# Cross attention heads woven into a causal attention's pairs, and PSUM values of two attentions copied by ScalarE

## What is computed

```python
x = _layernorm(x + _L0_attn_ref(x, ...))        # bucketed linear attention
x = _layernorm(x + _L0_xattn_ref(x, ctx, ...))  # two softmax attentions, 16 heads of 32, with feed-forward: "a1", "a2"
x = _layernorm(x + _L0_ffn_ref(x, ...))         # 16 experts, 4 chosen
x = _layernorm(x + _L1_attn_ref(x, ...))        # causal, 16 heads of 64: "l1"
x = _layernorm(x + _L1_xattn_ref(x, ctx, ...))  # cross attention, 16 heads of 8: "lx"
x = _layernorm(x + _L1_ffn_ref(x, ...))         # 8 experts, 2 chosen, with a capacity
```

## Time and profile before

| | us |
|---|---|
| median of 3 runs | 814.76 |
| lowest, highest | 813.08, 826.92 |
| the profiled execution | 812.73 |
| its span in the trace | 810.9 |
| TensorE's mean granted clock in it | 0.934 |

### The profile page before, as it was taken

How to read it: one execution, slowest core, us unless ns; L and a number is a source line. 1 busy time by engine, 2 the same in 40 slices (tenths; PEclk the granted TensorE clock), 3 DMA queues, 4 the chain that set the end, 5 groups by cost and what they waited for, 6 DMA issues and landing times.

```text
span 810.9 us, 16176 instructions
## 1 busy us (share of the span) xinstructions
PE 726.4 (90%) x5744; PEld 537.8 (66%) x5744; DVE 492.8 (61%) x1309; ACT 413.1 (51%) x1047; POOL 290.0 (36%) x398
## 2 busy tenths in 40 slices
PE   5559898899998999999999989989898899999986
PEld 3336476665756566699888877857576445667665
DVE  3557798877869588254543446545445658674653
ACT  2215357565665576754544448655563544454311
POOL 0013455554556467320000008333331555454300
PEclk9959799999999999899999999999999656899999
DMA  7563343624427374000000000001010520000000
GB/s 238 156 140 74 87 95 78 149 52 110 109 53 190 85 174 159 2 1 1 1 1 1 1 1 4 1 1 36 6 40 5 171 82 26 9 2 8 8 7 7
DMA packets 25174, 48.10 MB, mean 59 GB/s; under 512 B 7264, under 2 KB 14192, under 8 KB 25096
## 3 DMA queue, kind: packets, MB, share of 16 engines
q1 hardware_dynamic: 24376, 45.66, 21.9%
q10 hardware_dynamic: 720, 1.41, 0.5%
HBM read 17.49 MB, written 0.52 MB: 22 GB/s over the span
## 4 chain that ended last, share of the span: by engine, by line
PE 62%; DVE 15%; issue 10%; ACT 7%; POOL 3%; DMA 2%; SPq 1%; POOLq 0%; DVEq 0%; ACTq 0%
PE G L522 8%; PE SC L772 7%; PE SC L759 7%; PE SC L702 5%; PE G L563 4%; PE SO L745 3%; DVE shift_cols L1471 3%; PE SC L794 3%; PE G L871 3%; ACT causal_probs L1085 2%; PE SO L826 2%; PE SC L678 2%; PE G L527 2%; PE SM L719 2%; PE G L585 2%
## 5 line engine op out<-in xcount | busy, mean ns | idle before, releaser
L1100 ACT ACTIVATE exps<-SC 128x512 f32<-128x512 f32 x192 | 114.2, 596 | 112.6 <-PE SC L702 112.0
L1471 DVE TENSOR_REDUCE shift_cols<-SC 128x2 f32<-128x512 f32 x192 | 129.7, 683 | 35.5 <-PE SC L678 34.6
L1550 POOL TENSOR_TENSOR rstd<-variance,consts 128x2 f32<-128x2 f32 (+1 forms) x48 | 37.2, 775 | 286.6 <-DVE variance L1164 283.7
L1619 POOL TENSOR_TENSOR VB<-exps 128x256 f32<-128x256 f32 x128 | 95.0, 749 | 65.1 <-ACT exps L1100 64.4
L1074 ACT ACTIVATE hidden<-SC,cols 128x256 f32<-128x256 f32 x128 | 53.5, 470 | 66.3 <-PE SC L759 66.1
L1641 POOL TENSOR_TENSOR causal_probs<-causal_probs,inverse 128x256 f32<-128x256 f32 x64 | 51.6, 828 | 70.5 <-DVE inverse L1484 70.5
L1505 DVE SCALAR_TENSOR_TENSOR R<-SC,small,R 128x128 f32<-128x128 f32 x128 | 39.0, 346 | 55.6 <-PE SC L772 55.0
L1085 ACT ACTIVATE causal_probs<-SC,negmax 128x128 f32<-128x128 f32 (+1 forms) x128 | 52.2, 423 | 37.2 <-DVE negmax L1479 37.0
L702 PE MATMUL SC<-stacked_q,stacked_k 100*128 100x256 f32 x256 | 66.5, 343 | 4.5 <-DMA stacked_q<-shift_rows 3.0
L772 PEld LDWEIGHTS SC<-ffn_w,hidden 128*128 128x128 f32 x512 | 66.0, 192 | 5.3 <-issue 1.8
L678 PE MATMUL SC<-stacked_k,stacked_q 96*128 96x256 f32 x256 | 56.6, 308 | 12.7 <-DVE shift_cols L1471 7.4
(11 more groups left out here) (244 smaller groups left out, 1500.1 us busy)
## 6 DMA issues: line engine op xcount, KB each, us to landing
stacked_k<-k_hi SPq DMA_DIRECT2D x64, 128.0 KB, 2.3
stacked_q<-q_hi SPq DMA_DIRECT2D x64, 128.0 KB, 2.4
ffn_w<-in_ffn_w SPq DMA_DIRECT2D x16, 512.0 KB, 4.6
stacked_k<-k_lo SPq DMA_DIRECT2D x32, 128.0 KB, 2.4
stacked_q<-q_lo SPq DMA_DIRECT2D x32, 128.0 KB, 2.4
packed_k<-U SPq DMA_DIRECT2D x48, 32.0 KB, 1.9
packed_q<-YN SPq DMA_DIRECT2D x48, 32.0 KB, 1.9
a_weights<-in_a_li SPq DMA_DIRECT2D x3, 256.0 KB, 8.2
```

The source lines that it names most:

```text
L1100: fn(exps[:, n % EXPS, :, :].rearrange("p t q -> p (t q)"), SC[1][:, n % 2, :, :].rearrange("p t q -> p (t q)"), ACT.Exp, scale=ATTENTIONS ...
L1471: v.tensor_reduce(shift_cols[:, n // UNIT % 4, :, n % UNIT], SC[0][:, n % 2, :, :], axis=AX.X, op=ALU.max, negate=True).then_inc(head_max, 1)
L1619: v.tensor_tensor(kept[n % EXPS].rearrange("p t q -> p (t q)"), exps[:, n % EXPS, 0, :], exps[:, n % EXPS, 1, :], ALU.add).then_inc(kept_r ...
```

## The change

Pairs 0 to 17 (ALONE = 18) stay alone, one a slot from 203 on. lx begins at slot 221. Pair 18 stands in slot 221, pair 19 in 222 and from there a pair in every second slot up to pair 31 in 246, while lx has a head in every slot: heads 0 to 27 run beside pairs or their remains. `mix(0)` starts at slot 252 in place of 266, and the last slot is 331 in place of 345.

For this PSUM is divided anew. From pair 19 on, pairs use SC0 alone and wait for the exponentials of the pair before. Heads 0 to 27 use one bank of SC1 for products and the other for transposed products, so each waits for the head before it. Values of heads and pairs share SO in one ring. The sums of two key tiles go to two weight tensors of a2 that are no longer needed, the values of lx to new buffers VX with a cleared pad, and the outputs of its first two batches to HE. Batches 2 and 3 of l1 share one place for q and k, which are drawn at steps spread over the slots. The projections of l1 stand at slots 216, 224, 237 and 253 (before: 216, 224, 232, 240, one tile a slot); both tiles now come in one slot. `cross_in` stands at 219, 227, 240 and 256 (before 221, 229, 247, 263). ScalarE's table of exponentials is loaded at L1_AT and no longer at LX_AT; its loads are 22 in place of 23. The last experts come at slots 253 to 259.

The second part: the 16 value tiles of a1 and a2 are copied by ScalarE, at the same steps.

The diff, cut to its core:

```diff
 LAG = 3
 RING = LAG + 1
 TURNED = 4
...
-LX_AT = L1_AT + NB * PAIRS
+
+
+ALONE = 18
+LX_AT = L1_AT + ALONE
...
@@ -155,16 +159,45 @@
     return M0_AT + E0 * (b + 1) + UP_LAG
 
 
+def pair_slot(i):
+    return L1_AT + (i if i <= ALONE else 2 * i - ALONE - 1)
+
+
+def pair_of(slot):
+
+    return PAIR_AT.get(slot)
+
+
+def pair_values_slot(u):
+    i = 2 * u + 1
+    return pair_slot(i) + LAG + (2 if i < ALONE else 3)
+
+
+PAIR_AT = {pair_slot(i): i for i in range(NB * PAIRS)}
+VALUES_OF = {pair_values_slot(u): u for u in range(NB * PAIRS // 2)}
+
+
 def causal_in_at(b):
-    return settle_at(b) + 5 if b < 2 else L1_AT + PAIRS * (b - 1) + 1
+    return settle_at(b) + 5 if b < 2 else L1_AT + (10, 18)[b - 2]
+
+
+def causal_in_steps(b):
+
+    return ((0, 1, 2, 3), (6, 7)) if b < 2 else ((0, 2, 4, 6), (3, 5)) if b == 2 else ((0, 2, 6, 10), (4, 8))
+
+
+def causal_parts(b):
+
+    keys, vals = causal_in_steps(b)
+    return sorted(zip(keys + vals, range(6)))
...
-    return L1_AT + PAIRS * b + 18 if b < 2 else LX_AT + HEADS * (b - 2) + 12
+    return causal_out_at(b) + 3
 
 
...
@@ -336,6 +372,10 @@
             return v
 
         kept = [carve(VB[k // 4], 1024 + 256 * (k % 4), TT, P) for k in range(EXPS)]
+        added = [W[n][:, T * k:T * k + T] for n in ("a2_wq", "a2_li1", "a2_li2", "a2_li3") for k in range(2)]
+
+        def key_sum(n):
+            return kept[n % EXPS].rearrange("p t q -> p (t q)") if n < STACK_HEADS else added[n % EXPS]
 
         def values(s, t, lo, hi):
             w = HEADS * ATTENTIONS[s // NB]["d"]
...
@@ -354,6 +394,11 @@
         QT, OT = ([carve(work[b], at, T) for b in range(NB)] for at in (1500, 1760))
         HB = [carve(HE, 1024 * k, 4, T) for k in range(2)]
         HX = [carve(HE, 512 * k, 8, SLOT) for k in range(4)]
+        outputs_of = [OB[:, 0:4, :], OB[:, 4:8, :], carve(HE, 0, 4, T), carve(HE, 1024, 4, T)]
+
+        def outputs(s):
+
+            return outputs_of[s % 2 + (2 if s in (LX * NB, LX * NB + 1) else 0)]
 
         shifted0, expd0, combine0 = ([carve(small[b], at, TT, E0) for b in range(NB)] for at in (0, 32, 64))
         onehot0 = [carve(small[b], 96, TT, K0, E0) for b in range(NB)]
...
+        def score_bank(n):
+            return SC[1][:, 0, :, :] if STACK_HEADS <= n < WOVEN_END else SC[0][:, n % 2, :, :]
+
+        def turned_bank(n):
+            return SC[1][:, 1 if STACK_HEADS <= n < WOVEN_END else n % 2, :, :]
+
+        def pair_bank(i):
+            return SC[i % 2 if i < ALONE else 0]
+
+        def causal_place(b):
+            return min(b, 1)
 
 
 
...
@@ -660,8 +717,12 @@
                 def head_products(n):
                     s, U_, k = stream_of(n), n // UNIT, n % UNIT
                     if n == STACK_HEADS:
+                        pe.wait_ge(exp_ready, ALONE)
+                    elif STACK_HEADS < n < WOVEN_END:
+                        pe.wait_ge(head_max, n)
+                    elif n == WOVEN_END:
                         pe.wait_ge(exp_ready, NB * PAIRS)
-                    if n >= 2:
...
@@ -691,15 +752,19 @@
                         pe.wait_ge(choice_in, 16 * UNIT_SLOTS)
                     if k == 0:
                         pe.wait_ge(shifts_in[U_ % 4], 16 * (U_ // 4 + 1))
-                    if n >= 2:
+                    if STACK_HEADS < n < WOVEN_END:
+                        pe.wait_ge(head_exp, n)
+                    elif n >= 2:
                         pe.wait_ge(head_exp, n - 1)
+                    if n == WOVEN_END:
...
                     if n < STACK_HEADS:
                         q, kk = SQ[U_ % UNIT_SLOTS][:, k, :], SK[U_ % UNIT_SLOTS][:, k, :]
                     else:
                         r, c = slice(HD * k, HD * k + HD), U_ % 4
                         q, kk = LQ[s % 2][r, c, :], LK[s % 2][r, c, :]
                     for t in range(TT):
-                        last = mm(SC[1][:, n % 2, t, :], kk[:, t * P:(t + 1) * P], q, start=True, stop=True)
+                        last = mm(turned_bank(n)[:, t, :], kk[:, t * P:(t + 1) * P], q, start=True, stop=True)
                     last.then_inc(head_scores, 1)
 
                 ones = const("later_key")[:, P:P + HD]
...
@@ -780,18 +845,19 @@
                         for j in range(2):
                             wait_emptied(pe, ("up", NB * E0 - 1 - j))
                             wait_emptied(pe, ("down", NB * E0 - 1 - j))
-                    if c == 0:
-                        for m in range(4):
-                            wait_emptied(pe, ("k", L1 * NB + b, m))
-                            wait_emptied(pe, ("q", L1 * NB + b, m))
-                    if i >= 2:
+                    if c % 2 == 0:
+                        for side in ("k", "q"):
+                            wait_emptied(pe, (side, L1 * NB + b, c // 2))
+                    if i > ALONE:
+                        pe.wait_ge(exp_ready, i)
+                    elif i >= 2:
                         pe.wait_ge(exp_ready, i - 1)
...
@@ -815,9 +881,7 @@
                         for t in range(TT):
                             for h in range(2):
                                 wait_emptied(pe, ("v", s, t, h))
-                    if u == 0:
-                        wait_emptied(pe, ("O", STACK_HEADS // UNIT - 1))
-                    g = fill(pe, "pair", ("OC", u))
+                    g = fill(pe, "out", ("OC", u))
...
@@ -988,6 +1051,9 @@
                             g = wait_filled(act, (side, s, m))
                             fn(halves[side + "_hi"][:, 2 * m:2 * m + 2, :].rearrange("p a b -> p (a b)").bitcast(f32r),
                                g[:, :], ACT.Copy, scale=at["scale"] if side == "q" else 1.0).then_inc(hi_ready, 1)
+                    for t in range(TT):
+                        yield values_step(s) + t
+                        copied(("v", s, t), values(s, t, 0, 512), lambda g: g[:, :])
 
...
@@ -1111,10 +1177,10 @@
                         shifts_turned(unit_of(slot, TURN_AT))
                     if 0 <= slot - M0_AT < NB * E0:
                         gelu_up(slot - M0_AT)
-                    if slot == LX_AT:
+                    if slot == L1_AT:
                         nc.scalar.preload_act_table_set(EXP_AND_LN)
-                    if 0 <= slot - L1_AT < NB * PAIRS:
-                        pair_exponentials(slot - L1_AT)
+                    if pair_of(slot) is not None:
+                        pair_exponentials(pair_of(slot))
 
                 def back(slot):
...
@@ -1283,10 +1349,6 @@
                                 at["scale"] if side == "q" else 1.0,
                                 halves[side + "_hi"][:, two_of, :].rearrange("p a b -> p (a b)"),
                                 op0=ALU.mult, op1=ALU.subtract).then_inc(*emptied((side, s, m)))
-                    for t in range(TT):
-                        yield values_step(s) + t
-                        g = wait_filled(dve, ("v", s, t))
-                        v.tensor_copy(values(s, t, 0, 512), g[:, :]).then_inc(*emptied(("v", s, t)))
 
                 def after(s):
...
@@ -1493,7 +1552,7 @@
                     s = stream_of(UNIT * U_)
                     g = wait_filled(dve, ("O", U_))
                     dve.wait_ge(sums_inverse, U_ + 1)
-                    v.scalar_tensor_tensor(OB[:, 4 * (s % 2) + U_ % 4, :], g, -1.0, unit_inverse[:, U_ % 2, :],
+                    v.scalar_tensor_tensor(outputs(s)[:, U_ % 4, :], g[:, 0:T], -1.0, unit_inverse[:, U_ % 2, :],
                                            op0=ALU.mult, op1=ALU.mult).then_inc(*emptied(("O", U_)))
 
...
@@ -1614,9 +1674,7 @@
                 def add_key_tiles(n):
                     pool.wait_ge(head_exp, n + 1)
                     wait_filled(pool, ("O" if stream_of(n - EXPS) // NB == A1 else "S", (n - EXPS) // UNIT))
-                    if n == STACK_HEADS:
-                        wait_filled(pool, ("OC", 4 * NB - 1))
-                    v.tensor_tensor(kept[n % EXPS].rearrange("p t q -> p (t q)"), exps[:, n % EXPS, 0, :],
+                    v.tensor_tensor(key_sum(n), exps[:, n % EXPS, 0, :],
...
@@ -1732,7 +1790,7 @@
                 def cross_in(b):
                     s = LX * NB + b
                     for u in range(4):
-                        yield 1 + u if b < 2 else 2 + 4 * u
+                        yield 1 + u if b < 2 else 2 + 3 * u
                         wait_emptied(sp, ("kq", s))
                         if b >= 2:
...
@@ -1759,7 +1817,7 @@
                             sp.wait_ge(packed_cleared, 4)
                             sp.dma_start(LK[g][HD - 1:P:HD, :, :].bitcast(fp32).rearrange("p u t -> p (u t)")
                                          .rearrange("p (a c) -> p a c", c=P), ones).then_inc(key_ones_in, 16)
-                        if slot == LX_AT + 8 + 4 * g:
+                        if slot == pair_values_slot(NB * PAIRS // 2 - 1) + 1 + 2 * g:
                             wait_filled(sp, ("PT", NB * PAIRS - 1, 1))
                             wait_filled(sp, ("OC", 4 * NB - 1))
```

135 lines of the change are left out of this document (68 added, 67 removed).

## The result

Median 819.09 us after (813.81 to 826.69, 20 runs) against 812.88 us before (807.66 to 826.92, 20 runs): ratio 1.0081, 95% interval 1.0056 to 1.0105. The change makes the kernel about 6 us slower; forecast were 807.0 us and a gain. The time is inside the range (791 to 822) and within 2%, the direction is wrong. Now and then an execution is over 1.5% longer than the fastest of the same kernel; ratios, losses and remainders leave such executions out, medians don't.

A forecast was written before the change was run, and what follows sets the result against it. TensorE, busy 90% of the span, was taken as the bound. From 812.7 us: - 7.8 (slots 221 to 251) + 6.4 (moved work) - 3 (clock) - 1 (copies) = 807.3, given as 807 us; range 791 to 822, 8 in 10.

The forecast's parts named there:

- Slots 221 to 229: First woven slots: 38.5 us of TensorE work with waits plus 2.4 us before head 0 for packed rows, 41 us.
- Slots 230 to 247: Nine periods of one pair and two heads, set by a chain through ScalarE: 61.6 us, bounds 46 and 70.
- the plain periods: Periods in slots 230 to 247 without larger extra items: 6.0 us, or 6.1 with turned shifts.
- the second rival: Waits let the clock fall in the woven stretch, deciding below about 0.85: 825 us, chance 0.12.
- The three periods that hold more: In slots 230 to 247: 10.1 us with the projection, 8.0 with sums and compact keys, 7.0 with sums.
- A head's products about 0.22: Price in us at full clock for one head's products on TensorE; its transposed products the same.
- Slots 203 to 220: Stretch before the woven slots, forecast unchanged: 0 us.
- My sign for a wrong forecast: A change of more than 5 us in slots before 203, which the copies would then have made.
- Behind slot 252: Moved work adds 6.4 us, a higher clock in the 16 slots there saves 3 us (bounds 0 and 10).
- The copies: 16 value copies moved from VectorE to ScalarE: 1.7 us saved, 0.7 spent, 1 us gained.
- The first rival: TensorE's work decides and the clock stays up, pair scores under 5 us apart: 789 us, chance 0.22.
- The third rival: Each woven period waits for one more ScalarE copy, 0.6 to 0.8 us: 814 us, no change, chance 0.16.

The follow-up runs named there:

- e3: Kernel after with the two value tiles of batch 2 at steps 5 and 7, not 3 and 5; ratio to before 1.0029.
- e14: Kernel after with eight unread 512-column matmuls added ahead of head products, in woven slots where TensorE waits; ratio to before 1.0089.
- e2: Kernel after with the 16 value copies back on VectorE, so the weaving alone; ratio to before 1.0157.
- e1: Kernel before with only the 16 value copies moved from VectorE to ScalarE, nothing woven; ratio to before 1.0002.
- e15: Kernel after with turned halves in G and ahead of the transposed products, and batch 2's value tiles at steps 5 and 7; 805.85 us, ratio to before 0.9939.
- e20: Second measurement of e15's kernel, unchanged; 808.92 us, ratio to before 0.9943.

## Why the prediction was wrong

**Slots 221 to 229** were forecast at 41 us and took 40.9, with 2.8 us idle before head 0 against 2.4 forecast. The row names exponentials as the releaser, but this wait is for packed rows too:

```profile
545.38 1.87 SPq L1799 DMA_DIRECT2D packed_q<-YN  x3
...
547.63 0.21 ACT L1151 ACTIVATION_READ_ACCUMULATOR causal_probs<-SC,negmax 128x1 f32 x1
```

The last exponential was over at 547.84. The third of these DMAs, the first unit's sixth, was issued at 546.65 and takes 1.9 us to land: 548.55, and head 0 starts at 548.59. So the packed rows ended the wait, as forecast, but only its last 0.7 us are theirs: some 2.1 us would have gone to the exponentials anyway, which the forecast didn't see. That the size fits is partly luck.

**Slots 230 to 247, the step that failed.** Forecast 61.6 us, measured 71.3. The mechanism was right in the plain periods: of six, four are 6.3 us long and two 6.8, these partly at the low clock, and TensorE waits for ScalarE's exponentials before the transposed products (1.67 us in the row at 643.21). What failed is that all periods were priced at full clock, a term put at nothing, while the second rival named 0.85 as the point from which it decides; the clock was 0.81. The three periods that hold more took 12.5, 10.6 and 9.5 us against 10.1, 8.0 and 7.0, at clocks of 0.77, 0.68 and 0.54. At full clock the third took 6.9 us in e3, and the second 8.5 in e14; the first ran at full clock in neither (12.8 us at 0.76 in e3, 14.6 at 0.69 in e14, 14.7 at 0.62 in e2). By the windows the clock makes 71.3 - 63 = 8 us of the 9.7. A second term was mis-sized: "A head's products about 0.22" was read from the earlier trace rows, where two heads' products stand side by side. In the period the turned halves part them, each costs 0.43, and the chain is 3.95 + 0.60 + 0.1 + 0.43 + 0.78 + 0.43 = 6.3: 0.2 to 0.3 in a plain period, about 1 us in all. The second rival had the mechanism; it priced 15 us over nine periods at half clock throughout, and the clock was low in parts only.

**Slots 203 to 220** were forecast unchanged, without a look at how the moved tiles meet the projection. They took 5.1 us more: a second failed step, a term put at nothing. Slot 216 took 9.1 us against 3.8 before; e3 gives back 3.5 of it. The diff showed these neighbours beforehand. My sign for a wrong forecast, a change above 5 us before slot 203, looked in the wrong place.

**Behind slot 252** the forecast was +6.4 - 3 = +3.4 and the profile shows +4.7, near it by two errors that cancel. The last window of the earlier trace rows reaches head 48, 17 slots; the 16 that I took it for last 31.5 us at 0.63, and 35.9 us at 0.86 after. So 4.4 of the 4.7 us stand there, while the clock loss fell by 6.5 us, more than the 3 allowed for. The moved work and new waits cost some 11 us (4.4 + 6.5, an estimate), not 6.4; about 2 us of it is idle time of TensorE.

**The copies** were forecast at -1. e1 says 0 with 3 us of uncertainty; in woven kernels they are worth about 6 us, and no row says where.

**What didn't happen.** The first rival (periods under 5 us) would have needed the chain hidden; e15 shows that with both its halves mended a period still takes 5.1 us. The third rival gave 814 by a further copy of 0.6 to 0.8 us in each period; the four plain periods at full clock, 0.2 to 0.3 us over the forecast, have no room for it. Of the signs, pair scores 6 to 7 us apart and the wait before head 0 came, and so did the second rival's clock under 0.85; `mix(0)` came 120 us after pair 18, not 108 to 111.

As a whole, for the spans: the terms missed are 9.7 us in slots 230 to 247, 5.1 before 221, 1.3 behind 252 and 0.8 in slots 248 to 251, less 0.1 in slots 221 to 229 and 1.6 ahead of slot 203, in all 15.2 us. With the forecast of -5.4 that is the +9.8 of the profiled pair; the medians show +6. The profile of after has 58.6 us of clock loss where the mean of its runs has 49.4, so its parts are on the large side.

## What to carry to other kernels

Weaving two stages can trade one loss for another: here the clock loss fell by 10 us and the remainder rose by 16. Before it is judged, look in the woven order for every single-buffered bank and for what stands ahead of its release in the other engine's queue, since mending one of two such chains may show nothing while mending both does. Forecast the clock of a new mix of work as a term of its own, since a stretch priced at full clock was 8 us short here. And split the span of each timed run into clock loss and remainder: two versions with the same time may stand at very different points of that trade. But the split doesn't say what a lost us costs; that takes the same stretch at two clocks.

## What was not expected of the hardware

Products of two heads that use different rows of the array run interleaved when they are neighbours, 0.43 us for both (e20, 604.00 to 604.43), and take 0.43 us each when another matmul stands between (after, 643.21 and 644.44). The Trainium skill, page "TensorE: Matmul & The Clock Gate", section "Part 3: Packing small matmuls — row/col tiling", describes such concurrency for different row groups; the rows above agree.

The clock loss ahead of slot 203, where these kernels hardly differ, was 20.5 to 37.5 us between profiled executions. So a difference of a few us between the stage times of two profiles says little without the clock of each beside it: slots 230 to 247 took 67.8 to 74.1 us with the same code.
